# A language-model tower kernel: the order of TensorE's work laid out anew, and norms and unit vectors of q and k taken for two token tiles at once

## What is computed

```python
h = table.T[tokens] + bias
x = layernorm(h);  xn = layernorm(x) * norm_g + norm_b
q = xn @ Wq;  k, v = split(x @ Wkv)             # 16 heads of 64
k, v = [null_k; k], [null_v; v]                 # 2 extra keys: 2050 in all
q = q / |q| * q_scale;  k = k / |k| * k_scale   # per head
sim = 8 * q @ k.T - slope * distance;  causal mask
h = h + (softmax(sim) @ v) @ Wout
y = layernorm(h)
h = h + top-2-of-8 experts(y) + shared expert(y)
```

## Time and profile before

| | us |
|---|---|
| median of 3 runs (2959.22 to 2964.57) | 2959.45 |
| the profiled execution's own time | 2950.42 |
| its span in the trace | 2948.5 |
| PE busy | 2669.4 (91%) |
| DVE busy | 2104.4 (71%) |
| POOL busy | 1465.6 (50%) |
| ACT busy | 1373.1 (47%) |

### The profile page before, as it was taken

The page is one execution under the profiler, slowest core; times in us unless marked ns, Lnnn a source line. Parts: engine busy times, 40 slices in busy tenths (PEclk is TensorE's granted clock), DMA queues, the critical chain, the costliest instruction groups (busy, mean ns, idle before and its releaser), DMA issues. The chain is left out here.

```text
span 2948.5 us, 48293 instructions
## 1 busy us (share of the span) xinstructions
PE 2669.4 (91%) x13729; PEld 1323.7 (45%) x13729; DVE 2104.4 (71%) x5792; ACT 1373.1 (47%) x2924; POOL 1465.6 (50%) x1765
## 2 busy tenths in 40 slices
PE   3799989999989888999999999999997989999999
PEld 2443434344434444444444444444443436666666
DVE  6677777788787798788787878787877644444444
ACT  3455555565545465556564656555554431111111
POOL 6365746565766575656565666656564620000000
PEclk9799999999999999999999999999999889999999
DMA  1000001000100000000000010000002000000000
GB/s 45 15 23 16 23 16 26 16 24 14 44 23 24 16 23 14 23 16 24 16 23 16 24 25 14 24 16 24 17 18 76 14 8 1 1 1 29 1 1 29
DMA packets 123340, 59.10 MB, mean 20 GB/s; under 512 B 57936, under 2 KB 113872, under 8 KB 123088
## 3 DMA queue, kind: packets, MB, share of 16 engines
q1 hardware_dynamic: 121552, 51.84, 6.9%
q0 software_dynamic: 1536, 4.20, 0.5%
HBM read 34.33 MB, written 4.46 MB: 13 GB/s over the span
## 5 line engine op out<-in xcount | busy, mean ns | idle before, releaser
L673 POOL TENSOR_TENSOR acc<-acc,probs 128x512 f32<-128x512 f32 (+4 forms) x944 | 911.9, 966 | 208.7 <-ACT probs L760 123.9
L760 ACT ACTIVATE probs<-ps,btab 128x512 f32<-128x512 f32 (+4 forms) x1408 | 776.8, 589 | 424.2 <-PE ps L1196 263.9
L933 DVE CUSTOM_DVE_ANT_0 ps<-ps,tab_l 128x512 f32<-128x512 f32 (+1 forms) x896 | 566.0, 672 | 169.2 <-PE ps L1168 167.1
L1211 PE MATMUL ps<-probs,arena 128*64 128x512 f32 (+4 forms) x2816 | 636.1, 529 | 0.0
L1195 PE MATMUL ps<-arena 128*128 128x512 f16 (+4 forms) x1408 | 482.4, 343 | 23.7 <-ACT probs L760 10.7
L1196 PE MATMUL ps<-arena 128*128 128x512 f16 (+9 forms) x1408 | 479.5, 341 | 0.0
L1168 PE MATMUL ps<-arena 64*128 64x512 f16 (+4 forms) x1408 | 246.1, 343 | 121.9 <-DVE mx L933 114.5
L1048 DVE SCALAR_TENSOR_TENSOR h<-ps,wqkv,h 128x256 f32<-128x256 f32 x288 | 126.0, 479 | 292.6 <-PE ps L1272 292.6
L651 POOL TENSOR_SCALAR nsq<-ssq 128x4 f32<-128x4 f32 (+1 forms) x272 | 62.2, 229 | 472.4 <-DVE ssq L893 471.2
L654 POOL TENSOR_TENSOR rnorm<-nsq,minus_half 128x4 f32<-128x4 f32 (+1 forms) x272 | 282.7, 1039 | 22.8
L1140 PE MATMUL ps<-wqkv,xT 128*128 128x256 f32 (+1 forms) x1088 | 288.5, 389 | 0.0
(11 more groups left out here) (132 smaller groups left out, 3557.5 us busy)
## 6 DMA issues: line engine op xcount, KB each, us to landing
arena<-arena SPq DMA_DIRECT2D x512, 32.0 KB, 1.9
rl<-l_row SPq DMA_DIRECT2D x128, 128.0 KB
wqkv<-in_Wkv SPq DMA_DIRECT2D x32, 128.0 KB, 2.3
arena<-in_w SPq DMA_DIRECT2D x2, 2048.0 KB, 11.9
out<-h SPq DMA_DIRECT2D x8, 512.0 KB, 2.9
wqkv<-in_Wq SPq DMA_DIRECT2D x16, 128.0 KB, 2.4
arena<-augs SPq DMA_DIRECT2D x128, 1.0 KB
wo<-in_Wout SPq DMA_DIRECT2D x16, 128.0 KB, 2.1
```

The lines of the kernel that those rows point to most:

```text
L673: pool.tensor_tensor(a, probs[0:rows, (n - 2) % PB, 0:GW] if first else a, p, ALU.add).then_inc(sum_pool, 1)
L760: nc.scalar.activation(probs[0:rows, n % PB, 0:w], bank(S0 + n % 2)[0:rows, 0:w], ACT.Exp, bias=btab[0:rows, hh, z:z + 1]).then_inc(exp_do ...
L933: nc.vector.tensor_tensor_reduce(bank(A0 + hd)[:, 0:w], bank(A0 + hd)[:, 0:w], tab, 1.0, NEG, ALU.add, ALU.max, mx[:, hd, it, c:c + 1]).th ...
L1211: mm(bank(O0 + o % 2)[DH * hd:DH * hd + DH, c0:GW], vt[t % 2][0:rows, jt, hd, :], probs[0:rows, n % PB, 0:GW - c0], start=(jt == 0), stop= ...
```

## The change

Four things, all in one diff. **Order on PE:** `scores_a` is put on a grid of 2 units, due at 1.88 in a slot, `values` at 1.95 (were 0.5), `scores` at 0.0 and 0.1, and what goes through `turn_of` is kept 1.05 units apart. `sums`, `wout` and the stages before and after get other due times. **Two tiles at once:** `square` writes its squares for two token tiles into one buffer, `ssq_` and `inv_norm` are called once for two tiles, with 8 columns. **Unit vectors:** the product of k with the scales moves into `ssq_` as one instruction over both tiles, behind a wait for ACT's copies; `unit` is then one product over q and k of both tiles. **Buffer numbers** of `tqk` and `blk` now go on over the rounds.

```diff
 def turn_of(time):
-        apart = 0.65 if time < 0 else 0.9
+        apart = 0.65 if time < 0 else 1.05
-    LAGS = [dict(square=0.4, ssq=1.2, inv=1.9, unit=3.2, high=3.5, low=4.3, turn=4.8),
-            dict(square=0.9, ssq=2.0, inv=2.3, unit=4.2, high=5.0, low=5.8, turn=7.0)]
+    LAGS = [dict(square=0.3, ssq=1.05, inv=1.6, unit=2.2, high=3.5, low=3.9, turn=5.55),
+            dict(square=0.9, ssq=1.8, inv=3.2, unit=4.2, high=5.0, low=5.8, turn=7.0)]
 def project(t, t0, step):
-            at(s0 + lag["ssq"], "ssq", t, s)
-            at(s0 + lag["inv"], "inv_norm", t, s)
-            at(s0 + lag["unit"], "unit", t, s)
             if s % 2 == 1 or s == T:
                 g = s // 2
+                at(s0 + lag["ssq"], "ssq", t, g)
+                at(s0 + lag["inv"], "inv_norm", t, g)
+                at(s0 + lag["unit"], "unit", t, g)
-                halves[(t, g)] = s1 + 3.0
+                halves[(t, g)] = s1 + 2.2
-    def maxima(t, t0, step):
-        s0 = t0 - step
+    def maxima(t, first, step):
+        due = first - step
         for n in range(UNITS):
-            s0 = max(s0 + step, halves[(t, (units[n][0] + 1) // 2)])
+            due = max(due + step, halves[(t, (units[n][0] + 1) // 2)])
+            s0 = t0 + 2 * math.ceil((due - t0 - 1.88) / 2) + 1.88 if t > 0 else due
             at(s0, "scores_a", t, n)
-            at(s0 + 0.6, "max", t, n)
+            at(s0 + 0.0, "max", t, n)
-                at(s0 + 1.1, "shift", t, ig)
-                s1 = turn_of(s0 + 5.5)
+                at(s0 + 0.5, "shift", t, ig)
+                s1 = turn_of(s0 + 4.5)
-                at(s1 + 0.9, "keep_shift", t, ig)
+                at(s1 + 1.5, "keep_shift", t, ig)
 def attend(t, t0):
-            at(t0 + m - 0.9 * (m % 2) + 0.5, "exp", t, m)
-            at(t0 + m - 0.9 * (m % 2) + 1.85, "sum_p", t, m)
-            at(t0 + (m | 1) + 3.5, "values", t, m)
+            at(t0 + m - 0.9 * (m % 2) + 0.6, "exp", t, m)
+            at(t0 + m - 0.9 * (m % 2) + 2.0, "sum_p", t, m)
+            at(t0 + (m | 1) + 2.95, "values", t, m)
-            s0 = turn_of(t0 + 2 * last_block[ig] + 1 + 4.4)
+            s0 = turn_of(t0 + 2 * last_block[ig] + 1 + 3.75)
-            at(s0 + 0.9, "keep_l", t, ig)
-            at(s0 + 2.9, "inv_l", t, ig)
-            at(s0 + 6.1, "divide", t, ig)
+            at(s0 + 0.5, "keep_l", t, ig)
+            at(s0 + 3.4, "inv_l", t, ig)
+            at(s0 + 7.5, "divide", t, ig)
 def write(t):
-                w0 = turn_of(max(sums_at[(t, ig)] + 7.7, wout_from[0] + 2.4))
+                w0 = turn_of(max(sums_at[(t, ig)] + 10.9, wout_from[0] + 2.0))
-                at(w0 + 0.9, "add_o", t, ig, k)
+                at(w0 + 1.2, "add_o", t, ig, k)
-    project(0, -24, 1.7)
+    project(0, -24, 1.32)
-        project(t, t0 + PAIR * t - 74.0, 5.0)
+        project(t, t0 + PAIR * t - 77.5, 5.0)
-        maxima(t, t0 + PAIR * t - 35.0, 1.85)
+        maxima(t, t0 + PAIR * t - 42.0, 1.86)
-        embed(b, t0 + PAIR * (b * NP - 1) - 63.5, 10)
+        embed(b, t0 + PAIR * (b * NP - 1) - 60.5, 10)
-        gate(b, t0 + PAIR * (PAIRS - 1) + 1.0, 4.5)
+        gate(b, t0 + PAIR * (PAIRS - 1) + 8.0, 4.5)
-        sq = sb("sq", [128, 2, 256])
+        sq = sb("sq", [128, 512])
 def inv_norm(t, g):       # POOL, now 8 columns of two tiles
+                rows, cs = (128, slice(0, 8)) if g < PG - 1 else (NN, slice(4, 6))
 def square(t, s):         # ACT
-                need(act, ssq_ready, n - 1)
+                need(act, ssq_ready, PG * t + s // 2)
 def ssq_(t, g):           # DVE
+                dve.wait_ge(sq_ready, done)
                 nc.vector.tensor_reduce(ssq[...], sq[0:rows, DH * cs.start:DH * cs.stop]..., AX.X, ALU.add)
+                k = tqk[0:rows, (PG * t + g) % 2, 256:DH * cs.stop].rearrange("p (a d) -> p a d", d=DH)
+                dve.wait_ge(p_read, done)
+                nc.vector.tensor_tensor(k, k, scl...to_broadcast([rows, cs.stop - 4, DH]), ALU.mult).then_inc(k_scaled, 1)
 def unit(t, g):           # DVE
-                if s < T:
-                    nc.vector.tensor_tensor(q, q, rnorm...to_broadcast([rows, 2, DH]), ALU.mult)
-                for hd in range(2):
-                    last = nc.vector.scalar_tensor_tensor(out=k[:, hd, :], in0=k[:, hd, :], scalar=rnorm[...],
-                                                          in1=scl[0:rows, :], op0=ALU.mult, op1=ALU.mult)
+                dve.wait_ge(k_scaled, n + 1)
+                nc.vector.tensor_tensor(qk, qk, rnorm...to_broadcast([rows, cs.stop - cs.start, DH]), ALU.mult).then_inc(qk_read, 1)
```

More of the change, by code:

```diff
@@ L1 @@
+import math
 import concourse.bass as bass
@@ L241, in lm_tower_kernel @@
         attend(t, t0 + PAIR * t)
-        at(t0 + PAIR * t - 40.0 if t else -16, "tables", t)
+        at(t0 + PAIR * t - 46.0 if t else -16, "tables", t)
     for t in range(1, PAIRS):
-        project(t, t0 + PAIR * t - 74.0, 5.0)
+        project(t, t0 + PAIR * t - 77.5, 5.0)
     for t in range(1, PAIRS):
-        maxima(t, t0 + PAIR * t - 35.0, 1.85)
+        maxima(t, t0 + PAIR * t - 42.0, 1.86)
     for t in range(PAIRS):
@@ L411, in lm_tower_kernel @@
         rnorm_ready = sem("rnorm_ready")
+        k_scaled = sem("k_scaled")
         qk_read = sem("qk_read")
@@ L714, in square @@
                 act.wait_ge(proj_done, n + 1)
-                need(act, ssq_ready, n - 1)
-                nc.scalar.activation(sq[0:rows, s % 2, c0:256], p[0:rows, c0:256], ACT.Square).then_inc(sq_ready, 1)
+                need(act, ssq_ready, PG * t + s // 2)
+                nc.scalar.activation(sq[0:rows, :].rearrange("p (z u n) -> p z u n", z=2, u=2)[:, c0 // 128:2, s % 2, :],
+                                     p[0:rows, c0:256].rearrange("p (z n) -> p z n", n=128), ACT.Square).then_inc(sq_ready, 1)
                 need(act, pv_done, PAIR * (t - 1))
@@ L886, in null_unit, with ssq_ @@
                 nc.vector.tensor_tensor(null_blk[:, 0, :], null_k[:, :], null_blk[:, 1, :], ALU.subtract).then_inc(null_u_ready, 1)
-            def ssq_(t, s):
-                n = TK * t + s
-                rows, c0 = (128, 0) if s < T else (NN, 2)
-                dve.wait_ge(sq_ready, n + 1)
+            def ssq_(t, g):
+                n = PG * t + g
+                done = TK * t + min(2 * g + 2, TK)
+                rows, cs = (128, slice(0, 8)) if g < PG - 1 else (NN, slice(4, 6))
+                dve.wait_ge(sq_ready, done)
@@ L892, in ssq_ @@
                 need(dve, nsq_ready, n - 1)
-                nc.vector.tensor_reduce(ssq[0:rows, s % 2, c0:4], sq[0:rows, s % 2, 64 * c0:256].rearrange("p (a d) -> p a d", d=DH),
+                nc.vector.tensor_reduce(ssq[0:rows, (PG * t + g) % 2, cs], sq[0:rows, DH * cs.start:DH * cs.stop].rearrange("p (a d) -> p a d", d=DH),
                                         AX.X, ALU.add).then_inc(ssq_ready, 1)
-            def unit(t, s):
-                n, g = TK * t + s, s // 2
-                rows = 128 if s < T else NN
-                dve.wait_ge(rnorm_ready, n + 1)
-                dve.wait_ge(p_read, n + 1)
-                q, k = [tqk[0:rows, g % 2, 256 * z + 128 * (s % 2):256 * z + 128 * (s % 2) + 128].rearrange("p (a d) -> p a d", d=DH)
-                        for z in range(2)]
-                if s < T:
-                    nc.vector.tensor_tensor(q, q, rnorm[0:rows, s % 2, 0:2].unsqueeze(2).to_broadcast([rows, 2, DH]), ALU.mult)
-                for hd in range(2):
-                    last = nc.vector.scalar_tensor_tensor(out=k[:, hd, :], in0=k[:, hd, :], scalar=rnorm[0:rows, s % 2, 2 + hd:3 + hd],
-                                                          in1=scl[0:rows, :], op0=ALU.mult, op1=ALU.mult)
-                last.then_inc(qk_read, 1)
@@ new lines, in ssq_, with unit @@
+                k = tqk[0:rows, (PG * t + g) % 2, 256:DH * cs.stop].rearrange("p (a d) -> p a d", d=DH)
+                dve.wait_ge(p_read, done)
+                nc.vector.tensor_tensor(k, k, scl[0:rows, :].unsqueeze(1).to_broadcast([rows, cs.stop - 4, DH]), ALU.mult).then_inc(k_scaled, 1)
+            def unit(t, g):
+                n = PG * t + g
+                rows, cs = (128, slice(0, 8)) if g < PG - 1 else (NN, slice(4, 6))
+                dve.wait_ge(rnorm_ready, n + 1)
+                dve.wait_ge(k_scaled, n + 1)
+                qk = tqk[0:rows, (PG * t + g) % 2, DH * cs.start:DH * cs.stop].rearrange("p (a d) -> p a d", d=DH)
+                nc.vector.tensor_tensor(qk, qk, rnorm[0:rows, (PG * t + g) % 2, cs].unsqueeze(2).to_broadcast([rows, cs.stop - cs.start, DH]),
+                                        ALU.mult).then_inc(qk_read, 1)
@@ L1151, in turn @@
                                 o = 512 * z + 256 * s + 128 * hd
-                                last = tr(dst[:, z, hd, s, :], blk[:, g % 2, o:o + 128], ident16[:, :])
+                                last = tr(dst[:, z, hd, s, :], blk[:, (PG * t + g) % 2, o:o + 128], ident16[:, :])
                 else:
@@ L1155, in turn @@
```

(2 more changed lines are left out.)

49 lines of the change are left out of this document (24 added, 25 removed).

## The result

The change makes the kernel slower: **2998.69 us** (median of 4 runs, 2994.34 to 3007.39) against 2961.3 us on the same chip (4 runs, 2959.22 to 2964.57), ratio 1.0129 with a 95% interval of 1.0104 to 1.0154. Predicted were 2886 us and a range of 2838 to 2938. The time lies outside the range, and on the other side of no change.

The account below looks back on a forecast made before the run. PE was taken to bound the rounds, by its own stream and by late DVE. Stream -37, `wout` waits -31, shifts -7, maxima +10, clock -8 sum to -73: from 2959.5 to 2886 us, range 2838 to 2938.

Parts of the forecast that it names:

- The stream: PE's own work in the rounds: fewer shape changes and cheaper `wout` and `proj` save 2.4 us a round, -37 us.
- its waits for the division (-31): PE's `wout`, due later behind `sums`, no longer waits for divided outputs: 33.5 us of waits gone except 2.
- The three doubled places: Places where one `scores_a` directly follows another (units 1, 16, 30) and waits for DVE's maxima: 3.9 us a round.
- Failed step 1: POOL's inverse norms: two powers of 4 columns become one of 8, 1.06 to 2.12 us, at worst nothing.
- Failed step 2: DVE's `divide` moves from 6.1 to 7.5 units, so DVE stands less and the maxima behind come sooner.
- Failed step 3: New waits, chiefly DVE's `ssq_` for ACT's copy of the second tile: 0, bound 12 us of DVE a round.
- the slower rival: ACT's exponentials delay the copy `ssq_` waits for, 8 us a round reach `scores_a`: about 3005 us, chance 0.09.
- Failed step 4: PE's waits for DVE's maxima: 6.3 us a round against 5.6, +10 us, bounds -40 and +60.
- narrow slots: Slots at the narrow end wait perhaps 0.5 us for maxima, 4 to 8 a round: 2 to 3 us.
- Failed step 5: PE's granted clock: idle falls from 155 to about 125 us, so less half-speed time: -8, bounds -25 and 0.
- DVE takes back the most of it: Rival: narrow slots and doubled `scores_a` cost +40 to +60 instead of +10, 2915 to 2940 us, chance 0.14.
- Start and end ... 0: 3 `proj` and 3 `scores_a` move ahead of the first `scores`, out of round 0: 0, bounds -10 and +10.

Follow-up runs that it names:

- e1: Changed kernel with norms and unit vectors taken tile by tile as before and inverse norms due at 2.3: ratio 1.0115 to the kernel before, 2984.51 us.
- e2: Kernel before, its order kept, with norms and unit vectors for two tiles at once and inverse norms due at 3.2: ratio 1.0107, 2982.43 us.
- e8: Changed kernel with doubled `scores_a` one unit later, tables in two lots, last group's `divide` due at 10.2, `inv` still 3.2: ratio 0.9744, 2882.42 us.
- e10: Kernel before with only the inverse norms' due time changed, from 2.3 to 3.2: ratio 1.0144, 2987.93 us.
- e9: Changed kernel with only the inverse norms' due time put back, from 3.2 to 2.3: ratio 1.0002, 2948.61 us.
- e7: Kernel before, its order kept, with norms and unit vectors for two tiles at once and inverse norms due at 2.3: ratio 0.9865, 2922.67 us.
- e4: Changed kernel with `divide` of all groups due 8.7 instead of 7.5 units behind `sums`: ratio 1.0081 to the kernel before, 2972.58 us.
- e6: Changed kernel with `divide` of only the last group of a round due 10.2 instead of 7.5 units behind `sums`: ratio 1.0021, 2964.6 us.
- e5: Changed kernel with the second head's position tables made 3 units behind those of the first: ratio 1.0092 to the kernel before, 2986.16 us.
- e3: Changed kernel with the second `scores_a` of each doubled place one unit later: ratio 1.0016 to the kernel before, 2951.65 us.
- e13: Kernel before with inverse norms due at 3.2 and `unit`, `high`, `low`, `turn` 0.9 units later: ratio 1.0193, 3015.11 us.

## Why the prediction was wrong

**It failed at the places, not at the means.** The sum's largest terms held. The stream was to fall by 2.4 us a round and fell by 2.3 (-32 in 14 rounds). `wout` was to lose its waits for the division (-31) and did; the shifts' waits (-7) are gone. The rule of the Trainium skill (TensorE: Matmul & The Clock Gate, "What overlaps and what doesn't") by which the order would have cost 11 us is again not what the trace shows: with the order alone (e1) the stream is 126.1 us a round, with the old order (e2) 128.5. `wout` at 0.53 and `proj` near 1.4 were read above at 0.52 and 1.40. DVE was to be busy 16 us less a round and is 193 / 14 = 13.8 less; the difference is the product 512 wide, taken at 0.90 us from L971 and measured at 1.37, while the reduction (0.67) and the product of k (0.65, measured 0.60) fit. POOL's power of 8 columns, bounded by 1.06 and 2.12, takes 1.68. The three doubled places were priced at 3.9 us a round and cost 4.1. `values` at the first block of a group was named as next in line for the division, with up to 1 us a round: it took nothing in the changed kernel and 1.6 in e8.

**Failed step 1: POOL's place in the queue.** The prediction said of `inv_norm` "POOL is at 62% and this is at worst nothing". It costed the power's duration and passed over the due time, 2.3 to 3.2, which stood in the diff. e10, e9 and e7 against e2 show what this number alone is worth: 1.4, 1.3 and 2.4% of the time, more than half of the predicted gain in each case. The trace of before had it: POOL waited 394 us for squares' sums, and that was no waste but its place ahead of a row sum. The path it missed runs from POOL's row sum over DVE's stand at `unit` to the maxima: `scores_a` 34 waits 1.54 us a round with 3.2 and 0.10 with 2.3. With 2.3 the changed kernel is as fast as the one before (e9, 1.0002), though its other late places stay.

**Failed step 2: "DVE stands less before the landing, and the maxima queued behind it come sooner".** The move of `divide` was argued as a shorter wait alone. Its new neighbours weren't asked for: in the last group it lands just ahead of `low_`, and DVE's waits at `divide` rose, 87.1 to 98.8 us. The last `turn`'s 2.2 us a round had no term. e4 and e6 show the cause.

**Failed step 3: "New waits ... 0".** `ssq_` does wait for ACT now, 62.0 us in 14 times, but once a round behind the tables (4.4 us), not for p_read in each of nine calls, as the slower rival had it. And at the same point ACT holds up `scores` by 2.6 us. The tables' due time moved by 6 units, and the prediction didn't speak of it. e5 shows that the lump makes half of that wait or more; that the move by 6 units brought it about is argued and not shown.

**Failed step 4: the maxima, +10.** 5.6 us a round were to become 6.3. (The 83.6 us were divided by 15, but their rows cover 14 rounds: 6.0 us.) All waits of `scores_a` were 6.2 before and are 10.1. The doubled places (1, 16, 30) were right with 4.1, so the excess is in the other 6.1 us, where 2 to 3 were given to "narrow slots": they were priced with nothing on DVE but maxima. Number 29 (1.12) stands behind `divide`; 34 (1.54) and 24 (0.68) behind `unit`, as e9 shows: e4 and e6, which move `divide`, leave them as they are.

**Failed step 5: the clock, -8.** It was taken to follow the sum of idle time, and that sum was wrong; it came to +19 over the 14 rounds. The size isn't given by the sum either: e9 has 2.3 us more gaps a round than the kernel before, e8 0.8 us less, and the half clock is 9.5 and 2.7 against 6.3.

**The rivals.** The first, DVE takes back the most of it at "+40 to +60", is nearest in mechanism, and its size was right for the maxima (+57 us). It was short because two more places stood beside it and the clock turned on all three. The slower rival got the sign by another mechanism. "A first `scores` later than 125 us that round 0 does not give back" came true to the letter (125.1), and round 15 gave it back. Waits for maxima "over 150 us" did not quite: 140.8. DVE "idle ... for ACT's copy by more than 3 us a round" came true in size, 4.4 us, though it waits for ACT's squares and once a round.

With the places mended, the priced gain is there: e8 gives 0.9744, and -73 of 2959 would have been 0.975. That nearness is partly luck, since e8 holds e3's, e5's and e6's edits and a lower half clock than before.

"Start and end ... 0" came to -6 in the two profiled executions, of parts that were larger. Ahead of the first `scores` PE has 3 `proj`, 2 `turn` and 3 `scores_a` more to do, and waits 8.5 us for maxima (was 3.8) and 7.5 us for landings (was none): 10.8 us later (e2, e7 and e10, with the start of before, have them at 112.6 to 113.9). Round 15 is 18 us shorter: PE's gaps are 15.5 us (were 21.2), and its busy time at half clock is 9.0 us (was 27.1), half of which makes 9 us. No run takes these apart.

Open, and not tried: why the clock is so much better in round 15, what the move of the tables costs by itself, and what each of DVE's pieces in e13 costs.

## What to carry to other kernels

With in-order queues and written due times, price a move by its neighbours: for each moved piece, on each engine, list what it now stands ahead of and what it waits for, first of all on the engines that are not the bound. A wait on an idle engine can be a reservation worth keeping: POOL's 394 us were. And mend several late places together before judging an order: what one gives back the next can take up (e4), and the time at half clock fell much only with three of them mended (e8).
